# Cross-attention in a fused Perceiver block: six score chunks ahead of a head's first outputs, the merge as transposes, maximum rows copied by ScalarE, and one pair of chunks added by VectorE

## The reference, cut to what matters

```
q = _qdq(x) @ _qdq(wq).T + bq ;  k, v = split(cond @ wkv.T + bkv)      # 16 heads x 32
attn = softmax(einsum('bnhd,bmhd->bhnm', q, k) / sqrt(32), axis=-1)     # 256 x 4096 a head
o = einsum('bhnm,bmhd->bnhd', attn, v).reshape(B, N, C)
out = _qdq(o) @ _qdq(wp).T + bp
```

## Time and profile before

| | us |
|---|---|
| median of 3 runs | 627.62 (626.0 to 627.74) |
| the profiled execution, its own time | 625.34 |
| its span, first to last instruction | 623.5 |
| busy in the span: TensorE, its weight loads | 603.5, 482.0 |
| busy: VectorE, ScalarE, GpSimd | 369.4, 299.1, 228.4 |
| chain that ended last: TensorE's share | 88% |

### The profile page before, as it was taken

How to read it: one execution, slowest core, us unless ns; L and a number is a source line. 1 busy time by engine, 2 the same in 40 slices (tenths; PEclk the granted TensorE clock), 3 DMA queues, 4 the chain that set the end, 5 groups by cost and what they waited for, 6 DMA issues and landing times.

```text
span 623.5 us, 12623 instructions
## 1 busy us (share of the span) xinstructions
PE 603.5 (97%) x4455; PEld 482.0 (77%) x4456; DVE 369.4 (59%) x680; ACT 299.1 (48%) x424; POOL 228.4 (37%) x120
## 2 busy tenths in 40 slices
PE   8999999999999999999999999999899899999997
PEld 6877788888887677776777777776798789789996
DVE  3996530430434778887788788874764244376562
ACT  4444233233232555555555555555247678644451
POOL 2000200000002778887887888881100664410000
PEclk9999999999999999999999999999999899999999
DMA  8873644615639655556666555620032315145510
GB/s 292 310 238 121 188 171 160 202 67 161 208 102 280 172 152 151 147 155 158 159 158 157 147 147 147 157 83 2 1 136 69 136 67 202 69 159 199 187 63 34
DMA packets 29758, 92.19 MB, mean 148 GB/s; under 512 B 5472, under 2 KB 9568, under 8 KB 23008
## 3 DMA queue, kind: packets, MB, share of 16 engines
q1 hardware_dynamic: 28480, 89.67, 47.3%
q10 hardware_dynamic: 1248, 2.10, 0.9%
HBM read 65.02 MB, written 18.35 MB: 134 GB/s over the span
## 4 chain that ended last, share of the span: by engine, by line
PE 88%; DVE 4%; ACT 4%; issue 2%; POOL 1%; DMA 1%; POOLq 0%; SPq 0%; ACTq 0%; DVEq 0%
PE ps L340 16%; PE ps L341 16%; PE ps L342 16%; PE ps L1291 11%; PE ps L1388 10%; PE ps L1400 9%; PE ps L1414 4%; POOL p_sum L581 1%; PE ps L1374 1%; PE ps L1376 1%; ACT h_ring L772 1%; DMA f_ring<-stream 1%; PE ps L1273 1%; ACT probs L744 1%; PE ps L1364 1%
## 5 line engine op out<-in xcount | busy, mean ns | idle before, releaser
L700 ACT ACTIVATE p_ring<-ps 128x1024 f32<-128x1024 f32 x128 | 125.7, 1022 | 100.7 <-PE ps L1388 68.2
L961 DVE TENSOR_REDUCE m_part<-ps 128x1 f32<-128x512 f32 x240 | 150.5, 685 | 29.1 <-PE ps L1291 26.1
L581 POOL TENSOR_TENSOR p_sum<-p_sum,p_ring 128x1024 f32<-128x1024 f32 x60 | 142.8, 2380 | 9.1 <-ACT p_ring L700 4.8
L1291 PE MATMUL ps<-k_stack,q_max 96*128 96x512 f32 x240 | 86.7, 421 | 0.9 <-issue 0.6
L1388 PE MATMUL ps<-q_stack,k_stack 98*128 98x256 f32 x512 | 80.7, 286 | 0.2 <-ACT p_ring L700 0.2
L1388 PEld LDWEIGHTS ps<-q_stack,k_stack 98*128 98x128 f32 x512 | 74.8, 189 | 7.7 <-ACT p_ring L700 1.3
L1400 PE MATMUL ps<-p_ring,v_head 128*32 128x256 f32 x1024 | 71.6, 383 | 0.1
L1291 PEld LDWEIGHTS ps<-k_stack,q_max 96*128 96x128 f32 x240 | 40.9, 188 | 22.9 <-DVE m_part L961 12.7
L916 DVE SCALAR_TENSOR_TENSOR kl_buf<-ps,biases,kh_buf 128x512 fp32r<-128x512 f32 x32 | 23.6, 748 | 58.1 <-ACT kh_buf L661 57.8
L312 DVE TENSOR_TENSOR l_ring<-f_ring,h_ring 128x2048 fp32r<-128x2048 f32 x22 | 50.2, 2288 | 12.5 <-ACT h_ring L308 12.5
L340 PE MATMUL ps<-xt_h,h_ring 128*128 128x256 f32 x200 | 56.5, 282 | 0.0
(11 more groups left out here) (194 smaller groups left out, 1052.8 us busy)
## 6 DMA issues: line engine op xcount, KB each, us to landing
f_ring<-stream SPq DMA_DIRECT2D x29, 1024.0 KB, 4.9
k_stack<-kh_scratch SPq DMA_DIRECT2D x60, 256.0 KB, 4.6
kh_scratch<-kh_buf SPq DMA_DIRECT2D x32, 256.0 KB, 5.5
kl_scratch<-kl_buf SPq DMA_DIRECT2D x32, 256.0 KB, 5.9
v_head<-v_all SPq DMA_DIRECT2D x16, 512.0 KB, 3.0
k_stack<-kl_scratch SPq DMA_DIRECT2D x30, 256.0 KB, 4.2
v_all<-stream SPq DMA_DIRECT2D x4, 256.0 KB, 4.7
f_ring<-stream SPq DMA_DIRECT2D x4, 256.0 KB, 5.8
```

Of the source, the lines that this page charges most:

```text
L581: nc.gpsimd.tensor_tensor(p_sum[:, p, :], p_ring[:, 0, :] if n == 0 else p_sum[:, p, :], p_ring[:, c % 4, :], ALU.add).then_inc(sums_done, 1)
L700: nc.scalar.activation(p_ring[:, c % 4, :], ps[:, 2 * (c % 2):2 * (c % 2) + 2, :].rearrange("p b n -> p (b n)"), ACT.Exp, scale=XSCALE).th ...
L961: nc.vector.reduce_max(m_part[:, j // NT, j % NT:j % NT + 1], maximum_bank(j), AX.X).then_inc(max_read, 1)
L1291: nc.tensor.matmul(maximum_bank(j), q_max[p][0:SPLIT_ROWS, at128(j % NT)], k_stack[p][0:SPLIT_ROWS, j // NT * D:(j // NT + 1) * D], start= ...
```

## The change

- TensorE's order for a head becomes: S0, X3 X4, S1, X5 X6, S2, X7, S3, X8 X9, D, X10, S4, X11, S5, X12 X13, V0 V1 V2 V3, X14, S6, X15, X'0, S7, merge, X'1, V4 V5 V6, maximum rows, V7, X'2. The output of head h-1 is copied by ScalarE just before exponential 3 instead of 2.
- VectorE adds chunks 2 and 3 in a new tile `p_pair` (`add_pair`), between its reads of X10 and X11. GpSimd adds `p_pair` where it added chunk 2. Chunk 3 has no denominators on TensorE any more. Exponentials 6 and 7, which overwrite chunks 2 and 3, wait for that addition.
- The merge is 4 transposes of `o_t` into bank 6; VectorE adds the four bands with two reductions and then divides.
- `maximum_row` moves from VectorE to ScalarE, behind exponential 7 of the head before.
- The outputs' maxima are taken once over heads 0 to 13 and once for each of the last two, not per head.
- The maxima's banks and waits follow; `pick` and its set-up on GpSimd are gone.

```diff
-SUM_CHUNKS = (0, 1, 2, 4, 5, 6)
+SUM_CHUNKS = (0, 1, 3, 4, 5, 6)
+IN_SUM = SUM_CHUNKS + (2,)
-SUMS_BEFORE = (-2, -1, 0, None, 1, 1, 2, None)
+SUMS_BEFORE = (-2, -1, 0, None, 1, 1, None, None)
...
         def maximum_bank(j):
-            return bank((6, 4, 6)[j] if j < 3 else 5 if j == 15 else 4 + j % 3)
+            return bank((5, 4, 6)[j] if j < 3 else 4 + j % 3)
...
             def sum_chunks(h, p):
                 for n, c in enumerate(SUM_CHUNKS[1:]):
-                    pool.wait_ge(exp_done, 8 * h + c + 1)
+                    if c == 3:
+                        pool.wait_ge(pair_done, h + 1)
+                    else:
+                        pool.wait_ge(exp_done, 8 * h + c + 1)
...
             def exponentials(h, first=False):
                 for c in range(CHUNKS):
-                    if c == 2 and not first:
+                    if c == 3 and not first:
                         evacuate_output(h - 1)
...
+                    elif c >= 6:
+                        act.wait_ge(pair_done, h + 1)
...
             def normalize_output(h):
                 dve.wait_ge(merge_done, h + 1)
-                order.step(nc.vector.reciprocal(r_den[:], bank(4).rearrange("p (t c) -> p t c", c=64)[:, 0:NT, DH]))
+                groups = merge_bank().rearrange("p (u g d) -> p u d g", u=2 * NT, d=DH)
+                added = merge_bank()[:, N:N + NT * DH].rearrange("p (t d) -> p t d", t=NT)
+                order.step(nc.vector.tensor_reduce(den[:], groups[:, NT:2 * NT, 0, :], axis=AX.X, op=ALU.add))
+                order.step(nc.vector.tensor_reduce(added, groups[:, 0:NT, :, :], axis=AX.X, op=ALU.add))
+                order.step(nc.vector.reciprocal(r_den[:], den[:]))
...
+            def add_pair(h):
+                dve.wait_ge(exp_done, 8 * h + 4)
+                wait(dve, sums_done, NSUMS * (h - 1) + 2)
+                nc.vector.tensor_tensor(p_pair[:], p_ring[:, 2, :], p_ring[:, 3, :], ALU.add).then_inc(pair_done, 1)
...
-            def head(h, p, after=True):
+            def head(h, after=True):
-                chunk_maxima(h + 1, 3, 15)
-                if not first:
-                    normalize_output(h - 1)
-                chunk_maxima(h + 1, 15, 16)
-                negate_maximum(h + 1)
-                if not first:
-                    output_maximum(h - 1)
-                if after:
-                    chunk_maxima(h + 2, 0, 2)
-                maximum_row(h + 1, 1 - p)
-                if after:
-                    chunk_maxima(h + 2, 2, 3)
+                chunk_maxima(h + 1, 3, 11)
+                add_pair(h)
+                chunk_maxima(h + 1, 11, 16)
+                negate_maximum(h + 1)
+                if after:
+                    chunk_maxima(h + 2, 0, 1)
+                if not first:
+                    normalize_output(h - 1)
+                if after:
+                    chunk_maxima(h + 2, 1, 3)
...
             def merge(h, last_two=False):
-                    pe.wait_ge(max_read, 16 * (h + 2) + 13)
-                for t in range(NT):
-                    nc.tensor.matmul(bank(4)[:, 64 * t:64 * t + DH], o_t[:, at128(t)], pick[:, 0:DH],
-                                     start=True, stop=True)
-                    last = nc.tensor.matmul(bank(4)[:, 64 * t + DH:64 * t + DH + 1], o_t[:, at128(NT + t)],
-                                            pick[:, DH:DH + 1], start=True, stop=True)
+                    pe.wait_ge(max_read, 16 * (h + 2) + 15)
+                for t in range(2 * NT):
+                    last = nc.tensor.transpose(merge_bank()[:, at128(t)], o_t[:, at128(t)], ident[:])
...
-                if c not in SUM_CHUNKS:
+                if c not in IN_SUM:
                     last = denominators(p_ring[:, c % 4, :])
```

More of the change, by code:

```diff
@@ L555, in _ @@
                                         pattern=[[-1, P]], channel_multiplier=1).then_inc(consts_ready, 1)
[L556 to L561, removed]
             nc.gpsimd.memset(ones_col[:], 1.0).then_inc(ones_set, 1)
@@ L1004, in normalize_output, with output_maximum @@
                                                    scalar=r_den[:, t:t + 1], in1=bv_row[:, bass.ts(h, DH)],
                                                    op0=ALU.mult, op1=ALU.add).then_inc(o_done, 1)
-            def output_maximum(h):
-                dve.wait_ge(o_done, NT * h + NT)
-                order.step(nc.vector.tensor_reduce(a_part[:, :, h], o_all[:, :, bass.ts(h, DH)], axis=AX.X,
+            def output_maximum(part, first, last):
+                dve.wait_ge(o_done, NT * last)
+                order.step(nc.vector.tensor_reduce(a_part[:, :, part], o_all[:, :, first * DH:last * DH], axis=AX.X,
@@ L1038, in _ @@
                 order.leave(4, H // 2 - 2)
-            head(H - 3, 1)
-            head(H - 2, 0, after=False)
+            head(H - 3)
+            head(H - 2, after=False)
+            output_maximum(0, 0, H - 2)
             def add_last(n):
                 h, c = H - 1, SUM_CHUNKS[n + 1]
-                dve.wait_ge(exp_done, 8 * h + c + 1)
+                if c == 3:
+                    add_pair(h)
+                    dve.wait_ge(pair_done, h + 1)
+                else:
+                    dve.wait_ge(exp_done, 8 * h + c + 1)
@@ L1054, in _ @@
             normalize_output(H - 2)
-            output_maximum(H - 2)
+            output_maximum(1, H - 2, H - 1)
             for n in range(2, NSUMS):
@@ L1362, in maximum_rows @@
                 pe.wait_ge(negm_ready, NT * h + NT)
+                if not (isinstance(h, int) and h == H - 1):
+                    pe.wait_ge(max_read, 16 * h + 17)
                 for t in range(NT):
-                    last = nc.tensor.matmul(bank(5)[SPLIT_ROWS:SPLIT_ROWS + MAX_ROWS, at128(t)], neg_hl[:, t, :],
-                                            ident[:], start=True, stop=True)
+                    last = nc.tensor.matmul(maximum_row_bank()[:, at128(t)], neg_hl[:, t, :], ident[:],
+                                            start=True, stop=True)
                 last.then_inc(mrow_done, 1)
@@ L1430, in value @@
                     values(h, p, loads, c)
+                score(0)
                 next_maxima(3, 5)
-                score(0)
                 score(1)
                 next_maxima(5, 7)
+                score(2)
+                next_maxima(7, 8)
+                score(3)
+                next_maxima(8, 10)
                 if not first:
                     summed_denominators(h - 1, 1 - p)
-                next_maxima(7, 8)
-                score(2)
-                next_maxima(8, 9)
-                score(3)
-                next_maxima(9, 11)
-                for c in range(3):
+                next_maxima(10, 11)
+                score(4)
+                next_maxima(11, 12)
+                score(5)
+                next_maxima(12, 14)
+                for c in range(4):
                     value(c)
-                next_maxima(11, 13)
-                score(4)
-                next_maxima(13, 14)
-                score(5)
                 next_maxima(14, 15)
+                score(6)
+                next_maxima(15, 16)
+                if after_loads is not None:
+                    maxima(h + 2, p, after_loads, 0, 1)
+                score(7)
                 if not first:
                     merge(h - 1)
-                score(6)
-                next_maxima(15, 16)
-                score(7)
                 if after_loads is not None:
-                    maxima(h + 2, p, after_loads, 0, 2)
-                for c in range(3, 7):
+                    maxima(h + 2, p, after_loads, 1, 2)
+                for c in range(4, 7):
                     value(c)
```

59 lines of the change are left out of this document (36 added, 23 removed).

## The result

The changed kernel takes 628.69 us (median of 20 runs, 626.62 to 632.29), and the kernel before, on the same chips, 625.54 (20 runs, 623.67 to 627.82). The ratio is 1.0051, 95% interval 1.0036 to 1.0065: slower, by 3.2 us. The forecast was slower by 7.5 us, 635.1 in a range from 629.2 to 639.6. The three runs that the forecast started from had a median 2.1 above that of 20. One of the 12 executions of before_shift32 (experiment 1) took 846.52 us at a mean granted clock of 0.649 and is left out of its ratio.

What follows compares the result with a forecast made beforehand. TensorE was taken to bound the attention, with hardly any waiting. Steady heads 4.3, last head 3.4 and head 0 minus 0.2 gave plus 7.5 on 627.62: 635.1 us, range 629.2 to 639.6.

Steps and rivals of the forecast that it cites:

- The sign: Whole kernel: slower, chance 0.76, against 0.12 for faster and 0.12 for a change within 0.3%.
- the steady heads' term: Heads 1 to 14: each takes 15.07 us against 14.76, plus 0.31, so 4.3 us over 14 heads.
- The waits at X6, S3 and S5: TensorE in a steady head: added losses of 0.10 at X6, 0.20 at S3 and 0.79 at S5.
- head 0, -0.2: Head 0 has no D and no copy: minus 0.73 plus 0.3 and a later first row, about minus 0.2.
- TensorE has 14.6 us of work in 14.8: One head of the kernel before: TensorE hardly waits, so work added or removed shows in the time.
- The order of its queue is as before … no term: SyncE's loads of the keys' halves behind S3 and S7: they fit in 7.0 and 7.4 us, no term.
- the last head, +3.4: Head 15: 1.0 lost before D, 2.1 from D to the last D, 0.3 less merge, 0.65 more normalization: 3.4.
- a rival for the clock: TensorE's granted clock falls for a 2.8 us stretch, costing 1.4 us: 636.5; chance 0.02.
- GpSimd's last addition: GpSimd in a steady head: its four additions end 2.2 us into the next head, 0.5 to spare.
- The two cancel: Rival: no extra losses at X6 and S3, the last head costs 2: 628.6, up to 629.5; chance 0.12.
- The gain arrives: Rival: S5's wait is covered, head 14.28 us, whole kernel minus 3.5: 624.1; chance 0.12.
- The base: Starting time of the kernel before, the runs' median of 627.62 us, to which 7.5 was added.

Runs made afterwards that it cites:

- before_shift32: The kernel before with 32 unused bytes per partition ahead of `v_all`, giving later tiles the changed kernel's offsets modulo 64: 623.5 us, ratio 0.9955.
- experiment 1: 32 unused bytes ahead of `v_all`, in the kernel before (623.5 us, ratio 0.9955) and in the changed kernel (631.62 us, ratio 1.0089).
- experiment 4, b_transposes: The kernel before with only the merge as four transposes and two reductions, at the changed kernel's tile offsets: 624.63 us, ratio 0.998.
- experiment 5: Third key load of each half cut to 128 columns: on the kernel before with only the transposed merge, 622.75 us; on the changed kernel, 629.2 us.
- last_busy_9: The changed kernel with 9 products that nothing reads ahead of D in the last head: 628.18 us, ratio 1.0035.
- experiment 7: The changed kernel with D between S3 and X8 instead of behind X9: 623.88 us, ratio 0.9959.

## Why the prediction was off

The sign was right and the mechanism too: a chain from D over ScalarE's copy and exponential 3 takes more from TensorE than the removed work gives. The time was not. The forecast's plus 7.5 stands against plus 3.2. Added up from the profiles, with head 0 at full clock: -3.3 to the last copy of the values (199.03 and 195.77), -0.7 from there to head 1's maximum rows, +1.0 for 14 heads, +3.5 for the last head and +2.55 for its clock, +0.3 for the rest, together some 3.3. The two steps that failed most are the steady heads' term and the layout, which has no term. The last head's clock was left out too, and its cost hid part of the error of these two.

- **Missing step: where the tiles lie.** The forecast walked through every engine's instructions but took it that what the diff leaves alone stays as it is. The removed tile made it -2.5 to -3 (experiment 1). Only the steady heads' term was further off. The 768 products of 512 columns by 0.0067 (2.80 less 2.72, over 12) would be 5.1 us, but only 2.9 of it shows, between the copies at 74.95 and 189.72. Up to the first of these the difference is 0.2, in a stretch where TensorE also waits (it is busy for 18.06 of the 20 us from 40 to 60). Why the offset matters at all is not shown.
- **Mis-sized term: 14 heads, +4.3, measured +1.0.** The waits at X6, S3 and S5 came as laid out, to 0.03 us up to S5. The period was 14.83 on the mean and not 15.07, 0.24 less, 3.3 us in all: the largest single error. 0.16 of it is the merge, 0.36 where the transposes of the earlier trace rows gave 0.52: I had costed them from the durations of a row for which TensorE had waited, not from the start of what follows. Of the rest, some 0.08, nearly all shows by S7, which comes at 10.53 and not 10.6.
- **Mis-sized term: head 0, -0.2, measured about -0.7.** From the maximum rows of head 0 to those of head 1 it is 1.6 less at full clock, but part of that only moves: the changed kernel's first rows wait for a read of VectorE. From the last copy of the values to the rows of head 1 the kernel before takes 14.90, and the ten profiles of the changed order with a clock of 1.00 there take 14.03 to 15.39, with a median of 14.16.
- **Wrong reading of the kernel before: "TensorE has 14.6 us of work in 14.8: hardly any waiting, so what is added or removed shows".** Experiment 4 takes 0.4 of TensorE's work away and the head does not get shorter. The sum was right, the conclusion not: the keys' load cycle had nearly the same length, and VectorE's longer normalization stands right behind it (experiment 5). "The order of its queue is as before … no term" laid the load beside S3 to X'0 of the changed kernel (7.0 from the end of S3, measured 6.9; 7.48 from its start), where it fits. I did not lay it beside the kernel before, where 1.7 from S3 to the third issue (308.31 to 310.00) and 4.93 from there are all of the 6.62 from S3 to X'0.
- **Mis-sized term: the last head, +3.4, measured +6.0.** D came 4.82 behind the maximum rows, 3.47 before: 1.35 (forecast 1.0). At full clock the chain from D to the last D is 11.71, against 9.89: 1.82 (forecast 2.1). The normalization's tail gave 0.3. That makes 3.46, so these waits were sized well. The missing 2.55 is the clock, which fell behind the longer wait for GpSimd in every profile that has this wait; the median clock of 0.989 against 0.997 before points to most executions having it. The forecast had a rival for the clock at 0.02, priced at 1.4 us, with the transposes as its cause; the chance was too low, and the stretch was taken as 2.8 us long where 7 or 10 were measured. The clock was 1.00 from 216 to 420 with four transposes in each head, and it fell behind a wait of 2.2 us; last_busy_9, with the same transposes and the wait filled, kept it at 1.00. The rule that the forecast took from the Trainium skill (TensorE: Matmul & The Clock Gate, Part 4: PE-mode transpose) is not decided by that; four transposes in 14.8 us showed no effect.
- **Right:** GpSimd's last addition ends 2.6 into the next head (forecast 2.2) and holds nothing in a steady head; the bands' reduction takes 0.43 (0.42), the pair 1.23 (1.22), and VectorE's normalization holds nobody in the new order, though it does in the old one (experiment 5).
- **The rivals.** "The two cancel" gave 628.6, and that is the time measured, but by luck and not by its mechanism: the losses at X6 and S3 were there, the last head cost 6 and not 2, and the base was 2.1 too high. "The gain arrives" is false for the change, and nearly true for the order of experiment 7, where S5 waits 0.2 to 0.3 and the head is 14.45 (the rival said 14.28).
- **The base.** 627.62 was the median of three; that of 20 is 625.54.

## What to carry to other kernels

When a diff adds or drops a tile, work out the start of each large tile behind it and compare stretches of the trace that the diff does not touch; a control with the tiles moved back tells the layout from the change. A TensorE that is busy all the time may share its bound with a load cycle or an engine that paces it: before booking removed work as gain, follow each load from its release over all its issues to its first user. A filler experiment must be sized to the wait it fills, and a cost seen in one profiled execution should be looked for in the medians, and in the mean clock of each execution, before it is booked.

## What the runs showed of the hardware

- Twelve products of 128x512 fp32r take 2.80 us where the large tiles of SBUF start at a multiple of 64 bytes plus 32, and 2.72 where they start at a multiple of 64; both kernels, both ways.
- Four fp32 transposes between other products of a busy TensorE hold it for 0.36 us, 0.09 each, ahead of a maximum product (313.68 to 314.04, changed kernel) and for 0.41 ahead of a score chunk (310.02 to 310.43, b_transposes).
- The third of three 256 KB loads can be used 4.9 to 5.0 us behind its issue; a maximum product that waits for it is shown as "issue" in one kernel and as the DMA in another.
- From a TensorE wait of 2.2 to 2.8 us on, the granted clock was 0.50 for some 7 or 10 us in eight profiles of eight; with products that nothing reads in the wait (last_busy_9) it stayed at 1.00 in the profiled execution, with nothing else changed. 10 us at 0.50 in the last head cost 2.55 us. The clock also fell without such a wait: from about 198.8 to 202.2 in the changed kernel's profile and for some 10 us from 198.2 in that of before_shift32.
